# Every fourth product with C in the later batches' state scans moved from VectorE to GpSimd

## The reference, cut to what matters

```python
def step(state, xs):
    d_t, B_t, C_t, u_t = xs
    dA = jnp.exp(d_t[..., None] * A)
    state = state * dA + (d_t * u_t)[..., None] * B_t[:, None, :]
    y_t = jnp.einsum('ben,bn->be', state, C_t)      # sum over the 16 states
    return (state, y_t)
...
y = y + D[None, :, None] * u
y = y * jax.nn.silu(z)                              # z = layernorm(x)
```

## Time and profile before

| | us |
|---|---|
| median of 3 runs | 1851.22 |
| profiled execution | 1852.26 |
| its span, first to last instruction | 1850.5 |
| TensorE busy | 1763.2 |
| VectorE busy | 1300.1 |
| ScalarE busy | 963.8 |
| GpSimd busy | 666.5 |

### The profile page before, as it was taken

How to read it: one execution, slowest core, us unless ns; L and a number is a source line. 1 busy time by engine, 2 the same in 40 slices (tenths; PEclk the granted TensorE clock), 3 DMA queues, 4 the chain that set the end, 5 groups by cost and what they waited for, 6 DMA issues and landing times.

```text
span 1850.5 us, 19507 instructions
## 1 busy us (share of the span) xinstructions
PE 1763.2 (95%) x6114; PEld 809.9 (44%) x6114; DVE 1300.1 (70%) x1899; ACT 963.8 (52%) x1920; POOL 666.5 (36%) x696
## 2 busy tenths in 40 slices
PE   8999899879999999999999999999999899999999
PEld 4333344334444444444444444444444344445543
DVE  4989686989998689899787998987652444422221
ACT  7988786446545546566455566555435334320100
POOL 2434322337463324557222564562223333310000
PEclk9999899979999999999999999999999999999999
DMA  7999833767851146897212589732112799837110
GB/s 262 242 289 286 244 109 116 203 164 187 199 142 57 51 100 162 208 240 200 66 30 74 156 188 251 199 95 69 35 57 91 218 282 293 236 119 273 40 51 28
DMA packets 159045, 292.11 MB, mean 158 GB/s; under 512 B 18424, under 2 KB 51704, under 8 KB 156000
## 3 DMA queue, kind: packets, MB, share of 16 engines
q1 hardware_dynamic: 141664, 227.95, 39.0%
q0 software_dynamic: 17280, 62.92, 17.5%
HBM read 169.51 MB, written 58.26 MB: 123 GB/s over the span
## 4 chain that ended last, share of the span: by engine, by line
PE 72%; DVE 13%; ACT 6%; issue 4%; DMA 3%; POOL 1%; SPq 1%; DVEq 0%; ACTq 0%; POOLq 0%
PE p L846 11%; PE p L806 10%; PE p L823 9%; PE p L857 8%; PE p L893 6%; PE p L697 5%; DVE s_M L1025 5%; PE p L780 4%; PE p L829 4%; PE p L908 3%; PE p L746 3%; PE p L785 3%; DVE s_M L1020 2%; DVE s_M L1032 1%; DVE s_U L1178 1%
## 5 line engine op out<-in xcount | busy, mean ns | idle before, releaser
L1025 DVE TENSOR_TENSOR_SCAN s_M<-s_M 128x1024 f32<-128x1024 f32 x128 | 296.4, 2315 | 9.9 <-ACT s_M L1290 7.6
L1178 DVE CUSTOM_DVE_ANT_0 s_U<-p,s_U 128x512 f32<-128x512 f32 x256 | 188.2, 745 | 161.0 <-PE p L823 159.7
L823 PE MATMUL p<-s_U 128*128 128x512 f32 x512 | 268.2, 612 | 4.6 <-DVE s_U L1178 3.0
L806 PE MATMUL p<-s_U 128*128 128x512 f32 x512 | 256.7, 610 | 3.4 <-ACT s_U L1418 2.7
L1534 POOL DMA_DIRECT2D s_u<-s_M x120 | 111.7, 931 | 383.7 <-DVE s_M L1032 355.6
L1579 POOL TENSOR_SCALAR s_U<-s_U 128x512 f32<-128x512 f32 x256 | 231.9, 926 | 6.3
L857 PE MATMUL p<-s_U 128*128 128x512 f32 x512 | 223.7, 593 | 0.0
L846 PE MATMUL p<-s_U 128*128 128x512 f32 x472 | 216.0, 599 | 2.5 <-ACT s_U L1431 2.4
L1431 ACT COPY s_U<-p 128x512 f32<-128x512 f32 x196 | 105.5, 594 | 176.3 <-PE p L829 175.0
L1290 ACT ACTIVATE s_M<-s_dl,s_small 128x511 f32<-128x511 f32 x256 | 170.3, 717 | 35.5 <-DVE s_M L1025 35.3
L1426 ACT ACTIVATE s_U<-s_U 128x512 f32<-128x512 f32 x256 | 181.6, 710 | 5.3
(11 more groups left out here) (194 smaller groups left out, 2458.3 us busy)
## 6 DMA issues: line engine op xcount, KB each, us to landing
s_u<-s_M POOLq DMA_DIRECT2D x120, 512.0 KB, 7.6
s_bc<-bc_scratch SPq DMA_DIRECT2D x96, 256.0 KB, 4.5
k_scratch<-s_U SPq DMA_DIRECT2D x16, 1024.0 KB, 7.9
v_scratch<-s_U SPq DMA_DIRECT2D x16, 1024.0 KB, 5.4
s_U<-in_Wq SPq DMA_DIRECT2D x64, 256.0 KB, 6.6
s_U<-k_scratch SPq DMA_DIRECT2D x64, 256.0 KB, 5.4
s_U<-rk_scratch SPq DMA_DIRECT2D x64, 256.0 KB, 5.8
s_U<-in_Wo SPq DMA_DIRECT2D x64, 256.0 KB, 4.5
```

Source lines behind the costliest of these rows:

```text
L806: ins = e.matmul(banks[bk][:], wqq[j % 2][:, k, :], axT[b % 2][:, k, :], start=(k == 0), stop=(k == 3))
L823: e.matmul(banks[bk][:], qT[j % 3][:, k * 128:(k + 1) * 128], kT[j % 2], start=True, stop=True).then_inc(S["a_s"], 1)
L1025: e.tensor_tensor_scan(w, dA[i % 2], w, 0.0, ALU.mult, ALU.add).then_inc(S["m_s"], 1)
L1178: e.tensor_tensor_reduce(out=Pm[j % 2][:, k, :], in0=banks[ABANK[kind, j, k]][:], in1=rkb[j % 2], scale=rq[:, k:k + 1], scalar=-3.0e38, op ...
```

## The change

In batches 1 to 3, for `i` = 3, 7, ... 27 (7 half states of a batch, 21 in all), the product with C is made by GpSimd, after the scan's semaphore `m_s`. GpSimd waits for its own product (`m_cp`) and then issues the adding transfer. VectorE leaves these products out. The waits on `m_c` are counted anew (`vector_outs`, `pool_outs`), and SyncE waits for both counts before it reloads an `s_bc` tile. In the plan, such an `out` is 3.4 us of GpSimd, and every `out`, batch 0's too, now needs its `scan` to be done (0.15 us after its end). To free a semaphore, the small weight `dtw` now shares `d_ipw`.

```diff
+def on_pool(b, i):
+    return b > 0 and i % 4 == 3 and i < 2 * NS - 2
+def vector_outs(b, i):
+    return sum(not on_pool(a, k) for a in range(b + 1) for k in range(2 * NS if a < b else i + 1))
+def pool_outs(b, i):
+    return 32 * b + i + 1 - vector_outs(b, i)
...
-            part((kind, i), [("DVE", 1.25)] + ([("POOL", 0.8), ("SUM", 5.0)] if i < 2 * NS - 2 else []))
+            part((kind, i), [("POOL", 3.4), ("SUM", 5.0)] if on_pool(b, i) else [("DVE", 1.25)] + ([("POOL", 0.8), ("SUM", 5.0)] if i < 2 * NS - 2 else []), ("scan", i))
...
-                            e.wait_ge(S["d_ipw"], 16 * (b + 1))
+                            e.wait_ge(S["d_ipw"], 32 * (b + 1))
...
-                    elif kind == "out":
+                    elif kind == "out" and not on_pool(b, i):
...
-                        e.wait_ge(S["m_c"], 32 * b + i + 1)
+                        if on_pool(b, i):
+                            w = two(wy[s])
+                            e.wait_ge(S["m_s"], 32 * b + i + 1)
+                            e.tensor_tensor(w, w, rep(bcs[i // 2 % 2][:, 1, :], 2), ALU.mult).then_inc(S["m_cp"], 1)
+                            e.wait_ge(S["m_cp"], pool_outs(b, i))
+                        else:
+                            e.wait_ge(S["m_c"], vector_outs(b, i))
...
-                    if n >= 2 or b >= 2:
-                        e.wait_ge(S["m_c"], 2 * kk - 2)
+                    a, i = (b, 2 * n - 3) if n >= 2 else (b - 1, 2 * NS - 3 + 2 * n)
+                    if a > 0 or n >= 2:
+                        e.wait_ge(S["m_c"], vector_outs(a, i))
+                        if pool_outs(a, i):
+                            e.wait_ge(S["m_cp"], pool_outs(a, i))
```

More of the change, by code:

```diff
@@ L28 @@
 p_set c_act c_dve q_abs q_sum q_mm q_thr q_cut q_rnd q_put q_raw q_part q_row
-m_ip m_xp m_lo m_bc m_dt m_s m_yt m_xs m_u m_xd m_re m_sp m_da m_z m_ac m_dl m_dv m_h0 m_c m_hn m_g m_x m_rv m_rs
+m_ip m_xp m_lo m_bc m_dt m_s m_yt m_xs m_u m_xd m_re m_sp m_da m_z m_ac m_dl m_dv m_h0 m_c m_cp m_hn m_g m_x m_rv m_rs
 f_t f_g f_v f_ht f_o f_x f_th f_hc f_rv f_rs f_hn f_q f_z f_sc f_ob f_pad f_p f_h f_hq f_y
@@ L35 @@
 dve_own act_own pool_own
-d_w0 d_w1 d_w2 d_ipw d_dtw d_xpw d_const d_small d_c0 d_cr d_x0 d_x1 d_cb d_raw d_rows d_bcw d_bc0 d_bc1
+d_w0 d_w1 d_w2 d_ipw d_xpw d_const d_small d_c0 d_cr d_x0 d_x1 d_cb d_raw d_rows d_bcw d_bc0 d_bc1
 d_st0 d_st1 d_st2 d_st3 d_kw d_vw d_ks0 d_ks1 d_ks2 d_ksr d_rk
@@ L674, in pe_mamba @@
                             e.wait_ge(S["m_xd"], b + 2 if b else 1)
-                            e.wait_ge(S["d_dtw"], 16 * (b + 1))
                         bk = LBANK[b, "dt", i]
@@ L1615, in load_ipw @@
                 e.dma_start(ipw, A["ipwT"].rearrange("(t p) e -> p t e", p=128)).then_inc(S["d_ipw"], 16)
-                e.dma_start(dtw, A["dtwT"]).then_inc(S["d_dtw"], 16)
+                e.dma_start(dtw, A["dtwT"]).then_inc(S["d_ipw"], 16)
             def load_stage(w, c):
@@ L1672, in spread @@
                 def spread(n):
-                    kk = NS * b + n
-                    if n >= 2 or b >= 2:
-                        e.wait_ge(S["m_c"], 2 * kk - 2)
+                    a, i = (b, 2 * n - 3) if n >= 2 else (b - 1, 2 * NS - 3 + 2 * n)
[3 more added lines that the diff above has]
+                            e.wait_ge(S["m_cp"], pool_outs(a, i))
                     if n == 0 and b:
@@ L1693, in sp_mamba @@
                     elif kind == "add" and i == 2 * NS - 2 and b + 1 < NB:
-                        e.wait_ge(S["m_c"], 32 * b + 2 * NS - 1)
+                        e.wait_ge(S["m_c"], vector_outs(b, 2 * NS - 2))
                         e.dma_start(bcs[0][:], ctx_view(b + 1)).then_inc(S["d_cb"], 16)
```

## The result

The changed kernel takes 1889.0 us (median of 4 runs, 1887.63 to 1898.77), the kernel before, with a fourth run of it, 1850.4: 38.6 us slower by the medians, and a ratio of 1.0228 (95% interval 1.0184 to 1.0271). The forecast was 1862, the range ended at 1877. The profiled execution has a span of 1885.8 us, 35.3 more than before.

The account below looks back on a forecast made before the run. TensorE, busy 1763.2 of 1850.5 us, was taken as the bound where full, VectorE from 362 to 400 us. Terms summed to +10.7 us on 1852.26, 1863.0; the median being 1.0 lower, the forecast was 1862, range 1844 to 1877.

Parts of the forecast that it names:

- The last `w` tile, +7.8: Heads 17, 1 and 33's kind of place, one per batch: `w.3.3` and its twins come behind a scan, 2.6 us each.
- `rc` behind the product, +4.0: Heads 18 and 34: GpSimd's `rc` comes later behind the product, 2.0 us each, bounds 0 and 10.
- Ends of the mamba, 0: End of each batch's mamba: half state further, but half state 27's product ahead of `rc`; -1.0 to +1.0 each, taken 0.
- head 30, +1.0: Head 30: the product of half state 7 stands ahead of `rc` with like slack; +1.0 us, bounds 0 and 3.
- -1.2: Half state 3 of batches 2 and 3, preceding waits like that at 1061.71 us: -1.2 us each, between 0 and -1.7.
- My bound of 0 for a `mul` that is first: Shared SBUF access: each product costs VectorE between 0 (`mul` first) and 2.4 us (product first).
- The start, +1.5: Product 7 of batch 1 and its transfer delay batch 0's last layer norm deviations; +1.5 us, bounds 0 and 3.
- the keys' order at 0: The plan reorders the keys' stream up to the start; either sign, bounds -3 and +3 us, taken 0.
- What is given back, -3.6: TensorE's waits for VectorE around half state 3: -1.2 us in batch 1, -2.4 us in batches 2 and 3 together.
- Nothing is freed: Rival: VectorE's busy time falls by much less than 26 us as its operations stretch; no chance of its own.
- The product's time, 2.4 us: One 128 x 1024 product on GpSimd takes 2.4 us, between 1.28 and 3.9.
- every product blocks: Rival: the product is always first and VectorE idles, 1.2 us net for each of 21, 25 us; 1877 us, chance 0.14.

Follow-up runs that it names:

- the new order: The changed kernel's order on all engines; with the product on GpSimd it is the changed kernel itself, 1889.0 us.
- with fills: The changed kernel's order, each of GpSimd's 21 products replaced by fills of the same buffer, some 2.4 us that read nothing from SBUF: 1876.3 us, 1.0156.
- with nothing: The changed kernel's order, GpSimd's 21 products left out and an empty instruction signalling in their place: 1855.6 us, 1.0047.
- the two kernels with the `w` tile put back: The changed kernel, last `w` tile at three places taken between `mul` and scan (1886.5 us, 1.0196) or ahead of `mul` (1879.8 us, 1.0157).
- The need alone: The kernel before, with only the plan's need of every `out` for its scan added, all products staying on VectorE: 1858.2 us, 1.0049.
- the old order with nothing: The kernel before's order on all engines, the 21 products made by neither VectorE nor GpSimd: 1841.8 us, 0.9945.
- the old order: The changed kernel with the plan's line for `out` as before, so every engine keeps its earlier order; 21 products on GpSimd: 1867.2 us, 1.0108.
- the late three: Earlier order on all engines, GpSimd making only the products of half states 15, 23 and 27 of batches 1 to 3: 1861.7 us, 1.0057.

## Why the prediction was wrong

The direction was right (slower by more than the noise had a chance of 0.46), and so was the kind of mechanism: products that hold up VectorE and GpSimd's queue, and a `w` tile behind a scan. The sum was too small, 10.7 against 35.3 us in the profiled executions. By its steps, with the time at which ScalarE ends the exponentials of a head, less that in the kernel before, also for two kernels of the new order:

| up to head | 4 | 6 | 16 | 18 | 22 | 28 | 32 | 34 | 38 | end |
|---|---|---|---|---|---|---|---|---|---|---|
| changed | +0.4 | +6.7 | +3.1 | +9.6 | +15.4 | +15.1 | +20.3 | +26.8 | +33.8 | +35.3 |
| with fills | +1.1 | +2.5 | +6.7 | +8.4 | +13.9 | +13.6 | +13.2 | +14.7 | +23.1 | +26.2 |
| with nothing | +0.7 | +2.2 | -1.3 | +0.3 | +0.5 | +0.3 | -0.2 | +1.4 | +2.0 | +8.2 |

- *The last `w` tile, +7.8 (bounds 3.3 and 9.3).* This is the step that failed most. Heads 4 to 6, 16 to 18 and 32 to 34 give +6.3, +6.5 and +6.5, 19.3 in all; with fills or nothing they give 1.4 to 1.7 each, so some 5 us of each is reading SBUF. The delay was forecast at 3.1 us each for a product that starts first, and the wait came as 3.7. I then weighted it down to 2.6 and left out the clock behind it: half speed for most of 7 us, some 3 us more each. Nor does taking the wait away give all of it back, as the two kernels with the `w` tile put back show.
- *`rc` behind the product, +4.0.* The waits were 2.06 us each, as taken. But heads 18 to 22 and 34 to 38 lost 5.8 and 7.0 us. The rest is further `w` tiles (TensorE waits 1.67 us at 855.5 and 2.90 at 1218.6) and the clock (0.57 over 814 to 818 and 1176 to 1180 us); no step had them. This is the queue and not SBUF: with fills the same heads lost 5.5 and 8.4 us, with the same `w` waits of 1.68 and 2.91, and with nothing 0.2 and 0.6.
- *Ends of the mamba, 0, and head 30, +1.0.* Heads 28 to 32 lost 5.2 us, with fills or nothing none, so this is again reading SBUF: the scan of 4.32 us at 1058.22 above with the `w` tile behind it, and scans of 3.80 us at 1086.97 and 3.63 at 1095.10, behind which TensorE waits 2.38 us for an `s` tile at 1099.44. The first is due to the product of half state 3 of batch 3, for which the sum had -1.2, the one of 3.80 us to that of half state 7, for head 30. My bound of 0 for a `mul` that is first left out that the scan behind it can be held instead. At the end of batch 1's mamba TensorE waits 1.21 and 1.00 us for L1599 where it waited 1.00, which my bound of 1.0 for that place covers.
- *The start, +1.5 and the keys' order at 0.* The need alone made the wait for the earlier trace rows's tile 10 us instead of 5.6, and costs 9 us by the medians (1.0049). How much of that lies at the beginning stays open: that kernel's own execution was only 1.3 us behind at head 4. In the changed kernel's the longer wait was balanced up to head 4 by a shorter stop elsewhere (6.63 us at 200.9 us before, 2.50 at 217.8 after), and that stop differs from execution to execution: five other kernels with the old beginning waited 3.5 to 4.8 us there.
- *What is given back, -3.6.* The freed VectorE is worth 8.6 us if no product is made at all, more than I granted, but not where I looked: in the old order with nothing TensorE's waits of the earlier trace rows stood as before, 5.62 us at the beginning, and 1.97 and 1.75 us (at 707.66 and 1051.71). In the changed kernel VectorE's busy time did not fall, so the reason for this term was gone. "Nothing is freed" stood among my rivals as part of the slower cases, but not in the sum. Heads 6 to 16 did give back 3.6 us, as much as the whole term: that is luck. With nothing in the product's place they give 3.5, so it is the order, in which the 1.98 us of waiting at 714.87 is gone. (With fills they lost 4.2, with the waits of 2.60 and 1.55 us above.)
- *The product's time, 2.4 us*, was right: 2.34 to 2.37 us where it came first, 13 of 21 times, some 3.24 in 7 where `mul` was just ahead of it, and 2.55 in one.
- *The rival "every product blocks", 1877 us, chance 0.14*, was the nearest. Its rate of 1.2 us for each product was too high in the old order (18.2 us for 21, 0.9 each; 1.3 for the late three), and it lacked what the new order adds, 14 to 19 us with the product left out and 22 with it.

The rule of the Trainium skill, page "SBUF — State Buffer", section "Who interferes with whom", held for these products. The section calls the shared port pair "an exclusive lock". It says "for the whole instruction" beside VectorE's 2-port modes; the traces show the same for these operations, one engine kept out until the other's instruction ends (2.95 us for a `mul` of 1.2). The same section says that VectorE's two-input instruction contends with one of GpSimd "that reads SBUF, not with one that only writes it", as the fills show. Who goes next when an instruction ends is not settled by these runs: at 1057.14 us GpSimd went between `mul` and the scan, while at 1069.04 us before the change its operation of 3.41 us did not, though it too began while `mul` ran (1068.10, for 1.22 us). I had the rule and gave the case built on it 14%, on the argument that `mul` follows the scan without a gap. `mul` was ahead of the product in only 8 of the 21 places.

## What to carry to other kernels

Moving an elementwise operation with SBUF inputs from VectorE to GpSimd freed nothing here, as VectorE's neighbouring operations also have two SBUF inputs. Beside VectorE's `w` tiles, which come from PSUM, it disturbed nothing (0.72 and 0.75 us), so that is the place to look for. Splitting it into shorter ones made it worse, since GpSimd's queue was held for longer. Where TensorE is full, price a delay at its length less the slack, look at the clock behind it, and price a change of a planner's numbers as an edit of its own: here the order cost 14 to 19 us with the product left out.

## What the runs showed of the hardware

- Two products of 128 x 512 on GpSimd take 2.49 us as a pair when nothing comes between, but 3.47 us when a `mul` does; one of 128 x 1024 takes 2.35.
- A fill of 128 x 1024 takes 0.95 us on GpSimd and doesn't disturb a `mul` (1.21 us beside it). The time that it holds the queue still cost 10 and 21 us over 21 places.
- After a wait of 3.7 us TensorE's granted clock was 0.57 over 7 us, with TensorE busy for all of it. With the wait at 1.41 us or gone it was 1.00.
